# Windowed attention with its softmax divided before the weighting, one turn later, and reciprocal roots by Newton rounds on GpSimd

## The reference, cut to what matters

```
q, k, v = split(shift(x) @ Wqkv)               # 16 heads of 64
q = l2norm(q) * qs;  k = l2norm(k) * ks        # then rotated by position, with tables of cos and sin
sim = 8 * q . k  over the own 32-window and the one before it, masked
out = softmax(sim) @ v                         # per head: 32 queries x 64 keys
x = x + out @ Wo
x = x + (a * gelu(g)) @ W2 + b2,  a, g = split(layernorm(shift(x)) @ W1 + b1)
```

## Time and profile before

| what | value |
|---|---|
| median of 3 runs | 2470.04 us (2466.25 to 2470.73) |
| profiled execution, its own time | 2455.97 us |
| its span, first to last instruction | 2454.2 us |
| mean granted TensorE clock | 0.922 |
| busy share of the span | PE 82%, POOL 68%, DVE 67%, ACT 51% |

### The profile page before, as it was taken

One profiled execution on the slowest core, in us unless ns is written; L12 is line 12 of the kernel. 1 busy time (PEld: TensorE's weight loads), 2 busy tenths in 40 slices (PEclk: granted clock), 3 DMA queues, 4 the chain that ended last, 5 costly groups with the idle time before them and its releaser, 6 DMA issues.

```text
span 2454.2 us, 76245 instructions
## 1 busy us (share of the span) xinstructions
PE 2001.6 (82%) x33704; PEld 1355.8 (55%) x33800; DVE 1635.7 (67%) x1873; ACT 1246.8 (51%) x1330; POOL 1665.2 (68%) x992
## 2 busy tenths in 40 slices
PE   3678898588888888888888888888888888888885
PEld 1234443365656665656565666666565656565664
DVE  5556661576777677777776677667767776777664
ACT  1145455454555555555555555555555455545541
POOL 1000000998889887897888888878788889797851
PEclk7589999799999999999999899999999999999998
DMA  2311100122222222232222222222222223222221
GB/s 86 105 46 34 46 22 19 36 68 57 58 74 61 59 58 72 57 80 58 57 71 58 69 65 54 58 68 74 55 61 55 73 55 85 55 57 53 60 59 51
DMA packets 133726, 146.72 MB, mean 60 GB/s; under 512 B 60946, under 2 KB 76304, under 8 KB 132628
## 3 DMA queue, kind: packets, MB, share of 16 engines
q1 hardware_dynamic: 133396, 141.84, 23.0%
HBM read 30.83 MB, written 5.44 MB: 15 GB/s over the span
## 4 chain that ended last, share of the span: by engine, by line
PE 61%; DVE 13%; issue 11%; ACT 7%; POOL 4%; SPq 2%; DMA 1%; DVEq 0%; POOLq 0%; ACTq 0%
PE banks L472 10%; PE banks L481 7%; PE banks L554 7%; PE banks L571 5%; PE banks L537 5%; PE banks L498 4%; PE banks L519 4%; DVE arena L743 3%; PE banks L545 3%; PE banks L409 3%; PE banks L511 3%; ACT arena L988 3%; PE banks L580 3%; DVE arena L646 2%; PE banks L392 2%
## 5 line engine op out<-in xcount | busy, mean ns | idle before, releaser
L1095 POOL TENSOR_TENSOR arena<-arena,tab_sl 128x512 f32<-128x512 f32 x384 | 459.4, 1229 | 153.9 <-ACT arena L963 153.3
L1077 POOL TENSOR_TENSOR rn<-ss,minus_half 128x32 f32<-128x32 f32 x96 | 524.0, 5459 | 8.0
L1103 POOL TENSOR_TENSOR arena<-arena 128x1024 f32<-128x1024 f32 x192 | 450.4, 2369 | 68.9 <-DVE arena L790 68.9
L472 PE MATMUL banks<-w_qkv,arena 128*128 128x512 f32 x768 | 349.2, 598 | 9.4 <-ACT arena L955 9.4
L481 PE MATMUL banks<-ident,arena 128*128 128x128 f32 x1536 | 253.5, 332 | 109.2 <-DVE arena L790 75.9
L743 DVE TENSOR_TENSOR arena<-arena,rn 128x1024 f32<-128x1024 f32 x192 | 286.8, 1534 | 82.7 <-POOL rn L1077 82.6
L973 ACT COPY arena<-banks 128x1024 f32<-128x1024 f32 x96 | 97.9, 1020 | 444.1 <-PE banks L481 444.1
L537 PE MATMUL banks<-arena 64*32 64x64 f32 x12288 | 178.4, 227 | 141.5 <-issue 141.5
L481 PEld LDWEIGHTS banks<-ident,arena 128*128 128x128 f32 x1536 | 223.4, 174 | 124.1 <-DVE arena L790 80.7
L963 ACT COPY arena<-banks 128x1024 f32<-128x1024 f32 x192 | 194.2, 1012 | 182.9 <-PE banks L472 182.9
L646 DVE TENSOR_REDUCE arena<-banks 128x1 f32<-128x1024 f32 (+7 forms) x176 | 175.1, 1027 | 126.8 <-PE banks L373 126.5
(11 more groups left out here) (107 smaller groups left out, 3334.4 us busy)
## 6 DMA issues: line engine op xcount, KB each, us to landing
arena<-arena SPq DMA_DIRECT2D x1512, 64.0 KB, 2.0
w_qkv<-Wqkv SPq DMA_DIRECT2D x6, 1024.0 KB, 5.4
arena<-parts_dram SPq DMA_DIRECT2D x96, 48.0 KB
arena<-parts_dram SPq DMA_DIRECT2D x32, 144.0 KB
parts_dram<-arena SPq DMA_DIRECT2D x4, 768.0 KB, 3.3
w_o<-Wo SPq DMA_DIRECT2D x6, 512.0 KB
w_qkv<-Wqkv SPq DMA_DIRECT2D x6, 512.0 KB, 4.4
arena<-X SPq DMA_DIRECT2D x24, 128.0 KB
```

What stands on the lines that cost most here:

```text
L472: last = e.matmul(ps[:, BANK * c:BANK * (c + 1)], xsT[b][:, P * t:P * (t + 1)], w_qkv[:, at:at + BANK], start=True, stop=True)
L1077: e.tensor_tensor(rn[n % 2][:, :], ss[n % 2][:, :], minus_half[:, :], ALU.pow).then_inc(S["rn"], 1)
L1095: e.tensor_tensor(qk_sw[:, m, :].rearrange("p (h d) -> p h d", d=HEAD_DIM)[:, :, d:d + HALF], raw[:, m, :].rearrange("p (h d) -> p h d", d ...
L1103: e.tensor_tensor(to, to, qk_sw[:, m, :], ALU.add).then_inc(S["rs"], 1)
```

## The change

- **Weights divided in SBUF.** `normalise` multiplies the exponentials by the reciprocal sums in place, one instruction of 128x1024, before they are turned. The turned weights then give final outputs.
- **Values stationary.** In `gather` the 64x64 block of values is the stationary operand and 32 columns of weights move. The result comes out already turned, so `outputs_turn` and its PSUM pair are gone, and ACT copies the gather's result straight into the operand of `output`.
- **Order and depth.** PE begins a turn with score(s-3), then project(s), output(s-5), gather(s-4), turn(s-2), project_v(s-1), weights_turn(s-3). There is one turn more (107 in place of 106), q and k have three buffers in place of two, and weights and turned weights one in place of two. POOL rotates tile s-1 in turn s, and DVE's `norms` moves to s-1.
- **PSUM places** follow the new order: sc, proj, proj, wo, pv, tk, tq, v, pT.
- **Newton.** POOL makes the reciprocal root by an integer first guess and three Newton rounds: 14 dependent instructions of 128x32 in place of a clamp and a `pow`.
- **Moved.** The last window of keys is copied to the next tile's buffer by ACT from PSUM (before: POOL from SBUF, `keys_before`, L1112); the feed-forward gain goes from DVE to ACT; the semaphore for one row that is passed between halves is split off; `load_sin` comes after POOL's rotation.

The core of the diff:

```diff
@@ -293,29 +292,28 @@
                     place(("a_out", b), 3, "a_y", b + 1)
         last_on[3] = [("a_acc", a_groups)]
         turns.n = 0
-        FF = 8
+        FF = 9
         steps = n_tiles + FF + 2
         place(("xsT", 0), 4, "xs_ready", 2)
         for s in range(steps):
+            if 0 <= s - 3 < n_tiles:
+                place(("sc", s - 3), 4, "sub", s - 3 + 1)
             if s < n_tiles:
                 for m in range(2):
                     place(("proj", s, m), 4, "rc", 2 * s + m + 1)
+            if 0 <= s - 5 < n_tiles:
+                place(("wo", s - 5), 4, "x_attn", s - 5 + 1)
+            if 0 <= s - 4 < n_tiles:
+                place(("pv", s - 4), 4, "ot", s - 4 + 1)
             if 0 <= s - 2 < n_tiles:
-                place(("sc", s - 2), 4, "sub", s - 2 + 1)
+                place(("tk", s - 2), 4, "kp", s - 2 + 2)
+                place(("tq", s - 2), 4, "qt_ready", s - 2 + 1)
+            if 0 <= s - 1 < n_tiles:
+                place(("v", s - 1), 4, "v_ready", s - 1 + 1)
             if 0 <= s - 3 < n_tiles:
-                place(("pv", s - 3), 4, "o_norm", 2 * (s - 3) + 2)
-            if 0 <= s - 1 < n_tiles:
-                place(("tk", s - 1), 4, "kt_ready", s - 1 + 1)
-                place(("tq", s - 1), 4, "qt_ready", s - 1 + 1)
-                place(("v", s - 1), 4, "v_ready", s - 1 + 1)
-            if 0 <= s - 2 < n_tiles:
-                place(("pT", s - 2), 4, "pt", s - 2 + 1)
-            if 0 <= s - 3 < n_tiles:
-                place(("oT", s - 3), 4, "ot", s - 3 + 1)
+                place(("pT", s - 3), 4, "pt", s - 3 + 1)
             if s % GROUP == GROUP - 1 and s + 1 < n_tiles:
                 place(("xsT", (s + 1) // GROUP), 4, "xs_ready", 2 * ((s + 1) // GROUP) + 2)
-            if 0 <= s - 4 < n_tiles:
-                place(("wo", s - 4), 4, "x_attn", s - 4 + 1)
             G, k = (s - FF) // GROUP, (s - FF) % GROUP
             if s >= FF and k == 0 and G > 0:
...
             def weights_turn(n):
                 ps = pair("pT", n)
-                w.wait_ge(S["ex"], n + 1)
+                w.wait_ge(S["p_norm"], n + 1)
                 for c in range(CHUNKS):
...
             def gather(n):
@@ -527,23 +525,17 @@
...
-                    half, i = divmod(c, CHUNKS // 2)
-                    at = P * i + HEAD_DIM * half
+                for c in range(CHUNKS // 2):
                     for hp in range(2):
                         r = slice(64 * hp, 64 * hp + 64)
                         for i in range(WPT):
                             q = slice(WINDOW * i, WINDOW * (i + 1))
-                            last = e.matmul(ps[q, BANK * hp + HEAD_DIM * c:BANK * hp + HEAD_DIM * (c + 1)],
-                                            PT[n % 2][r, c, q], Vw[n % 3][r, i, at:at + HEAD_DIM], start=True, stop=True)
+                            at = BANK * hp + P * c + WINDOW * i
+                            for half in range(2):
+                                d = HEAD_DIM * half
+                                last = e.matmul(ps[d:d + HEAD_DIM, at:at + WINDOW], Vw[n % 3][r, i, P * c + d:P * c + d + HEAD_DIM],
+                                                PT[r, CHUNKS // 2 * half + c, q], start=True, stop=True)
                 last.then_inc(S["pv"], 1)
-
-            def outputs_turn(n):
-                ps = pair("oT", n)
-                w.wait_ge(S["o_norm"], 2 * n + 2)
-                for c in range(CHUNKS):
-                    last = e.transpose(ps[:, P * c:P * (c + 1)], O[n % 2][:, P * c:P * (c + 1)], ident)
-                last.then_inc(S["oT"], 1)

             def output(n):
...
             shift_in(0)
             for s in range(steps):
+                if 0 <= s - 3 < n_tiles:
+                    score(s - 3)
                 if s < n_tiles:
                     project(s)
+                if 0 <= s - 5 < n_tiles:
+                    output(s - 5)
+                if 0 <= s - 4 < n_tiles:
+                    gather(s - 4)
                 if 0 <= s - 2 < n_tiles:
-                    score(s - 2)
+                    turn(s - 2)
+                if 0 <= s - 1 < n_tiles:
+                    project_v(s - 1)
                 if 0 <= s - 3 < n_tiles:
-                    gather(s - 3)
-                if 0 <= s - 1 < n_tiles:
-                    turn(s - 1)
-                    project_v(s - 1)
-                if 0 <= s - 2 < n_tiles:
-                    weights_turn(s - 2)
-                if 0 <= s - 3 < n_tiles:
-                    outputs_turn(s - 3)
...
             def normalise(n):
-                ps = banks[:, pair_of["pv", n], :].rearrange("p (hp f i d) -> p hp f i d", hp=2, f=2, d=HEAD_DIM)
-                rs = rs_o[n % 2][:, :].rearrange("p (f i hp) -> p hp f i", f=2, hp=2)
-                to = O[n % 2].rearrange("p (i hp f d) -> p hp f i d", hp=2, f=2, d=HEAD_DIM)
-                w.wait_ge(S["pv"], n + 1)
                 w.wait_ge(S["recip"], n + 1)
-                w.wait_ge(S["oT"], max(0, n - 1))
-                for hp in range(2):
-                    e.tensor_tensor(to[:, hp], ps[:, hp], rs[:, hp].unsqueeze(3).to_broadcast([P, 2, CHUNKS // 2, HEAD_DIM]),
-                                    ALU.mult).then_inc(S["o_norm"], 1)
+                e.tensor_tensor(PB, PB, rs_o[n % 2][:, :].unsqueeze(2).to_broadcast([P, HEADS, 2 * WINDOW]), ALU.mult
+                                ).then_inc(S["p_norm"], 1)

             def subtract(n):
                 sc = banks[:, pair_of["sc", n], :].rearrange("p (h k) -> p h k", k=2 * WINDOW)
...
-                w.wait_ge(S["pT"], max(0, n - 1))
-                w.wait_ge(S["sm"], max(0, n - 1))
-                e.tensor_tensor(PB[n % 2], sc, mx_t[:, :].unsqueeze(2).to_broadcast([P, HEADS, 2 * WINDOW]), ALU.subtract
+                w.wait_ge(S["pT"], n)
+                w.wait_ge(S["sm"], n)
+                e.tensor_tensor(PB, sc, mx_t[:, :].unsqueeze(2).to_broadcast([P, HEADS, 2 * WINDOW]), ALU.subtract
                                 ).then_inc(S["sub"], 1)

...
                 w.wait_ge(S["tab_c"], l + 1)
-                w.wait_ge(S["tk"], max(0, n - 1))
-                w.wait_ge(S["tq"], max(0, n - 1))
+                w.wait_ge(S["tk"], max(0, n - 2))
+                w.wait_ge(S["tq"], max(0, n - 2))
...
                 if ff_here and k == 2:
                     ff_norm(G)
+                if 0 <= s - 3 < n_tiles:
+                    subtract(s - 3)
+                if 0 <= s - 1 < n_tiles:
+                    norms(s - 1)
+                if s < n_tiles:
+                    rotate(s)
+                if 0 <= s - 3 < n_tiles:
+                    sums(s - 3)
+                    normalise(s - 3)
                 if 0 <= s - 1 < n_tiles:
                     scale(s - 1)
-                if s < n_tiles:
-                    rotate(s)
-                if 0 <= s - 2 < n_tiles:
-                    subtract(s - 2)
-                if 0 <= s - 3 < n_tiles:
-                    normalise(s - 3)
-                if s < n_tiles:
-                    norms(s)
-                if 0 <= s - 2 < n_tiles:
-                    sums(s - 2)
-                if 0 <= s - 4 < n_tiles:
-                    residual(s - 4)
+                if 0 <= s - 5 < n_tiles:
+                    residual(s - 5)
                 if s >= FF and k == 0 and G > 0:
                     ff_residual(G - 1)
                 if ff_here and k == 1:
                     ff_stats(G)
-                if ff_here and k == 2:
-                    ff_gain(G)
                 if ff_here and k == 3:
                     ff_gate(G)
...
             def turn(n):
+                l, b, t = of_tile(n)
+                tk = banks[:, pair_of["tk", n], :].rearrange("p (c q) -> p c q", q=P)
                 w.wait_ge(S["tk"], n + 1)
                 w.wait_ge(S["sc"], max(0, n - 1))
-                w.wait_ge(S["kp"], n)
-                e.copy(KT[n % 2][:, :, WINDOW:WINDOW + P], banks[:, pair_of["tk", n], :].rearrange("p (c q) -> p c q", q=P)
-                       ).then_inc(S["kt_ready"], 1)
+                e.copy(KT[n % 2][:, :, WINDOW:WINDOW + P], tk).then_inc(S["kt_ready"], 1)
+                w.wait_ge(S["sc"], n)
+                if (n + 1) % tiles:
+                    e.copy(KT[(n + 1) % 2][:, :, 0:WINDOW], tk[:, :, P - WINDOW:P]).then_inc(S["kp"], 1)
+                else:
+                    e.memzero(KT[(n + 1) % 2][:, :, 0:WINDOW]).then_inc(S["kp"], 1)
                 w.wait_ge(S["tq"], n + 1)
-                w.wait_ge(S["sc"], n)
                 e.copy(QT.rearrange("p c q -> p (c q)"), banks[:, pair_of["tq", n], :]).then_inc(S["qt_ready"], 1)
...
             for s in range(steps):
+                if 0 <= s - 3 < n_tiles:
+                    exponents(s - 3)
                 if s < n_tiles:
                     project(s)
-                if 0 <= s - 1 < n_tiles:
-                    turn(s - 1)
+                if 0 <= s - 4 < n_tiles:
+                    outputs(s - 4)
```

(70 more changed lines are left out.)

51 lines of the change are left out of this document (17 added, 34 removed).

## The result

The changed kernel takes 2851.76 us (median of 4 runs, 2846.74 to 2860.33) against 2468.14 for the kernel before: a ratio of 1.1562, 95% interval 1.1524 to 1.16, slower by 15.6%. Forecast were 2885 us, between 2600 and 3020. The profiled execution took 2846.74 us with a span of 2844.9.

A forecast was written before the change was run, and what follows sets the result against it. A closed ring through PE, DVE and POOL was taken to bound the changed kernel: turns of 24.7 us against 20.37 over 95 turns, 411 us, plus 10 for the drain, +421 us, giving 2885 us, range 2600 to 3020.

The forecast's parts named there:

- The ring: PE's project_v waits for DVE's residual, behind scale, POOL's rounds, norms, subtract and score: 21.4 us a plain turn; chance 0.64.
- the signs that the prediction names: project_v waiting 4 to 6 us every turn, clock near 0.8, scale 3.4 or more, no gather stall, turns 24 to 26.5.
- Newton: POOL's 14 dependent instructions on 128x32 for the root: 4.9 to 5.0 us, against 5.9 for what is removed.
- lower bound for the rounds: POOL's Newton rounds at 2.7 us, if the fixed part were nothing but the hop and 0.1.
- Taking turns at SBUF: DVE's and POOL's SBUF instructions alternate: normalise costs the rounds up to 1.2 us, scale takes 3.5 instead of 2.35.
- The clock: PE stands 6.0 us, its clock falls, and project_v and weights_turn take 2.1 us more a turn; from below 0.
- the four kinds of turn: Turns k=0 to 3, by their feed-forward part: 24.1, 24.9, 24.6 and 26.5 us; mean 25.0 over 87 turns.
- The gather: PE's 128 matmuls: 1.8 to 3.9 us, 1.8 taken; its 1.8 us stall should go; both hidden in PE's wait.
- The 10 us for one turn more: One turn more in the drain, estimated at half a turn: 10 us.
- The clock staying up: Rival: longer PE work before the wait keeps the clock up, 2.1 us a turn falls away: 2690 us; chance 0.13.
- cheap rounds: Rival: Newton rounds take 2.7 us and don't collide with DVE, turns average 21.8 us: 2616 us; chance 0.12.
- Faster: Rival: x_attn comes before PE reaches v, so POOL's 18.4 us a turn bounds: 2290 us; chance 0.08.

The follow-up runs named there:

- experiment 1: Changed kernel with DVE's residual(s-5) moved to right after rotate(s), no longer behind scale(s-1): 2442.42 us, ratio 0.9927 to the kernel before.
- experiment 6: Changed kernel with POOL's rotation of the next tile waiting until both passes of scale are done: 2800.56 us, ratio 1.1369 to the kernel before.
- experiment 5: Changed kernel with four unused float32 products of 512 columns added on PE ahead of project_v: 2760.45 us, ratio 1.1209 to the kernel before.
- The fastest version: Changed kernel with residual early, first_values late, group statistics ahead of scale and group normalisation behind normalise: 2231.31 us, ratio 0.9059 to the kernel before.
- experiment 2: Changed kernel with POOL's first_values moved from before its rotation to after its Newton rounds: 2721.88 us, ratio 1.106 to the kernel before.
- experiments 3 and 11: 3: changed kernel with residual early and first_values late, 2339.57 us. 11: the same plus group statistics before scale, group normalisation after normalise, 2231.31 us.
- experiment 4: Changed kernel with clamp and one pow in place of the Newton rounds: 2936.38 us, ratio 1.1938 to the kernel before.
- experiment 8: Kernel before with the divided form alone (stationary values, no outputs_turn), close to the old order, pow and depth kept: 2736.98 us, ratio 1.1103.

## Why the prediction was right

**The ring** was the cause, as forecast: experiment 1 opens it at one place and takes off 409 us, where the change had cost 384. The steps of a turn of k=3 from score's start, forecast and measured (means over the trace, the score's from the turn shown): score 1.8 and 2.15; norms 6.6 and 6.9; rounds 12.8 and 12.3; scale 16.3 and 15.2; v free 16.7 and 15.4; end of the turn 26.5 and 24.8. Of the signs that the prediction names, the wait of project_v came in every turn between 1000 and 1900 us, though it was 3 to 8 us, and 16 in every eighth, and the granted clock fell to 0.86 and not near 0.8 (430 to 2760 us).

**Newton** was priced at 4.9; undisturbed it takes 4.45 (1391.99 to 1396.44), as the scalar forms take 0.22 and not 0.30 (the products take the 0.25 that was put). With normalise among them they take 5.3 us, in 80 of 96 turns, where 6.1 were forecast. The prediction's lower bound for the rounds, 2.7, would take 2.2 off a turn and not the 1.6 that it says. Against `pow` it gains, 85 us here and 25 in the kernel before.

**Taking turns at SBUF.** Normalise cost POOL 0.85 of the 1.2 forecast. Scale was put at 3.5 in turns of k=0, 2 and 3; it took 2.4 in k=0, 3.6 in k=2 and 2.8 in k=3 on average. In k=0 nothing runs beside it, as POOL's next work is ff_bias, which waits for DVE; the prediction has that wait, and missed that it frees scale in the turn before. Experiment 6 shows that taking turns counts: 51 us, of which the two passes' shorter mean (2 x 0.17 us a turn) makes 33; where the rest comes from is not shown.

**The clock.** 2.1 a turn was the estimate. In the turn shown project_v and weights_turn took 5.3 for 2.6, so 2.7; experiment 5 gives back 91 us, a lower bound, as its work doesn't fill the longer waits. The term alone is not measured. From v free to the next score the four kinds of turn took 7.0 us on average, against 6.9 forecast with the 2.1 in it.

**The gather** costs 2.52 us for 1.95 before, within the 1.8 to 3.9 given (1.8 was taken), and lies ahead of a wait of 3 us or more. The stall in it is gone, and its place is hidden in the same way: the page has 0.1 us of idle time in all ahead of L536's matmuls and puts 0.8 us to issue ahead of its weight loads, where 69.1 us stood in 900. The Trainium skill's figure for a weight load ("TensorE: Matmul & The Clock Gate", "LDWEIGHTS (loading the stationary operand)") gives, as an estimate, 6.8 us for 128 loads of 64 columns one after another; 2.52 us were measured for loads and matmuls together, so here it is no serial cost. The fastest version, where PE is 93% busy, is where both should count; no run shows it.

**Where two errors offset one another.** Mean turns from one score to the next (starts of L486 in the trace) were, for k=0 to 3, 33.3 or 23.0, 24.1, 22.1 and 24.8, against 24.1, 24.9, 24.6 and 26.5. So ordinary turns were put 1.5 us too high, most of all in k=2, by 2.5: ff_norm did not slow POOL's rotation (4.33 us for its four passes, as the 4.28 of the earlier trace rows), so the rounds began at 7.5 and not at 9.0. All of the 1.5 lies ahead of v: v was free 1.6 us earlier than forecast on average, by the rounds and by scale. The 10 us for one turn more did not come either: 95 turns of 4.12 us more make 391, which is all that the profiled executions differ by. Without `first_values` the forecast would have stood against 2722 (experiment 2), 163 us too high. The 130 us of `first_values` were not in it at all: I had read the change's list of POOL for what is queued behind the rounds, and not for what waits ahead of the rotation. That the time is right to 1.2% is partly luck.

**The rivals.** The clock staying up and cheap rounds gave 2690 and 2616; neither came. "Faster" named its point rightly: x_attn before PE reaches v. Experiment 1 moves it there, and the time ends below the kernel before, but at 2442, not 2290: POOL's and the feed-forward part's order took over, which experiments 3 and 11 then remove.

## What to carry to other kernels

When buffers are handed out round robin, write down for each place whose reader frees it, and where that reader stands in its own engine's list: here a stage of 0.28 us behind a stage that waits for another engine closed a ring over the whole turn; the change cost 384 us with it, and moving it gave 409. Check every wait of a reordered list against the new place of what it waits for, the rare ones too (one memset in eight turns, 130 us). And a form with less work can need another order on each engine before it pays: the divided form cost 11% close to the old order and nothing that can be told with exp early, and with its own order and four stages moved, the whole change is 9.4% faster. How much of that the moves would give the kernel before by themselves was not tested.

## What the runs showed of the hardware

- `pow` on 128x32 for 5.46 us did not keep DVE's SBUF-to-SBUF pass waiting (1.22 to 1.23 us in 62 turns, experiment 4), while products of 128x512 on POOL and such a pass take turns: two passes of scale took 3.3 us beside the rotation and 2.4 apart from it (experiment 6). What lets the pass by during a `pow` was not tested.
- More work on PE made a kernel faster: 335 us of products whose result nobody reads took 91 us off, as the granted clock rose from 0.858 to 0.922.
- 64x64 stationary with 32 columns moving: 128 float32 matmuls in 2.52 us, against 1.95 for 64x32 with 64 moving.
- Score and gather one after the other, 256 small matmuls, stall for 1.8 us each time, 39 times in 900 us, put down to nothing but issue; 5.3 us apart, the stall is gone (0.1 us of idle time in the whole run). With the new gather right behind score (experiment 8) it stays, 44.7 us in 34 waits between 1000 and 1900 us.
